# Associative scan of a hybrid layer: VectorE steps without two SBUF operands, part of the score sum on VectorE, TensorE reordered, and chunks shifted from SBUF to SBUF

## What is computed

```
def _combine(left, right, W):              # LANES = 4, hd = 32
    q = left.reshape(B, T, LANES, hd)
    k = right.reshape(B, T, LANES, hd)
    v = ((left + right) @ W).reshape(B, T, LANES, hd)
    scores = einsum('btld,btmd->btlm', q, k) * hd ** (-0.5)
    att = softmax(scores, axis=-1)
    z = einsum('btlm,btmd->btld', att, v)
    z = _rms_norm(z) / (1.0 + arange(LANES))[None, None, :, None]
    return left + z.reshape(B, T, C)

d = 1
while d < T:                               # 11 shifts: 1, 2, 4, ... 1024
    shifted = concatenate([identity rows (B, d, C), x[:, :-d]], axis=1)
    x = _combine(shifted, x, W)
    d *= 2
```

## Time and profile before

| | |
|---|---|
| time, median of 3 runs | 2099.97 us (2096.91 to 2100.51) |
| time of the profiled execution | 2098.23 us |
| its span | 2096.5 us |
| busy in the span | TensorE 1715.4 (82%), VectorE 1421.2 (68%), ScalarE 970.7 (46%), GpSimd 688.0 (33%) |
| the scan's sections, 1304.4 to 1898.5 | 44, with three to drain |

### The profile page before, as it was taken

How to read it: one execution, slowest core, us unless ns; L and a number is a source line. 1 busy time by engine, 2 the same in 40 slices (tenths; PEclk the granted TensorE clock), 3 DMA queues, 4 the chain that set the end, 5 groups by cost and what they waited for, 6 DMA issues and landing times. The chain is left out here.

```text
span 2096.5 us, 44156 instructions
## 1 busy us (share of the span) xinstructions
PE 1715.4 (82%) x14662; PEld 1126.9 (54%) x14662; DVE 1421.2 (68%) x2559; ACT 970.7 (46%) x2157; POOL 688.0 (33%) x498
## 2 busy tenths in 40 slices
PE   5699989998998999899974565899999999994374
PEld 3234333333333433334344554888888888884373
DVE  7777777777787777777624125688888888884222
ACT  4166666776676677676632112233333333332120
POOL 5300000000000000000013432677777777763532
PEclk9599999999999999999965786999999999997587
DMA  3200000000000000000007215122222222212523
GB/s 109 77 17 18 17 11 17 18 17 11 18 17 11 18 17 17 11 17 18 2 21 245 72 46 147 31 81 80 80 80 80 80 80 80 80 50 82 192 69 101
DMA packets 171652, 117.20 MB, mean 56 GB/s; under 512 B 10940, under 2 KB 161852, under 8 KB 171208
## 3 DMA queue, kind: packets, MB, share of 16 engines
q1 hardware_dynamic: 167368, 106.33, 17.3%
q0 software_dynamic: 4096, 8.46, 1.1%
HBM read 63.98 MB, written 50.72 MB: 55 GB/s over the span
## 5 line engine op out<-in xcount | busy, mean ns | idle before, releaser
L557 DVE TENSOR_REDUCE chunk_max<-ps_max 128x1 f32<-128x512 f32 (+3 forms) x1280 | 698.5, 603 | 211.2 <-PE ps_max L663 123.3
L606 ACT ACTIVATE probs<-ps_s 128x512 f32<-128x512 f32 (+3 forms) x1280 | 599.6, 547 | 317.2 <-PE ps_s L655 163.8
L636 PE MATMUL ps_s<-Qs,Ks 50*128 50x512 bf16 (+3 forms) x1280 | 379.3, 357 | 70.7 <-DVE chunk_max L557 50.7
L646 PE MATMUL ps_max<-Ks,Qs 48*128 48x512 bf16 (+3 forms) x1280 | 385.8, 360 | 13.1 <-POOL a_ident L499 10.5
L706 PE MATMUL ps_o<-probs,Vp 128*32 128x512 f32 (+3 forms) x2560 | 349.9, 571 | 11.4 <-ACT O_sb L589 11.1
L514 POOL TENSOR_TENSOR A_b<-A_newton,b_tile 128x128 f32<-128x128 f32 x32 | 14.6, 455 | 917.5 <-ACT A_newton L613 917.5
L1424 POOL TENSOR_TENSOR lane_products<-L,q 128x1024 f32<-128x1024 f32 x132 | 309.5, 2376 | 4.0 <-DMA L<-scanned 4.0
L636 PEld LDWEIGHTS ps_s<-Qs,Ks 50*128 50x128 bf16 x1280 | 103.1, 94 | 311.2 <-DVE chunk_max L557 247.1
L1479 DVE TENSOR_TENSOR weighted<-exp_scores,psV_s 128x4096 f32<-128x4096 f32 x44 | 194.2, 4413 | 0.2 <-issue 0.2
L1437 POOL TENSOR_TENSOR q<-L,z_normed 128x1024 f32<-128x1024 f32 x44 | 141.6, 3218 | 144.7 <-DVE z_normed L1459 144.7
L1558 PE MATMUL psS<-ident,lane_products 128*128 128x128 f32 x1408 | 169.4, 279 | 23.7 <-POOL lane_products L1424 23.7
(11 more groups left out here) (224 smaller groups left out, 2375.0 us busy)
## 6 DMA issues: line engine op xcount, KB each, us to landing
scanned<-q SPq DMA_DIRECT2D x44, 512.0 KB
L<-scanned SPq DMA_DIRECT2D x44, 512.0 KB
m_w<-in_L_ffn_w_dram SPq DMA_DIRECT2D x32, 512.0 KB
Qs<-q_parts SPq DMA_DIRECT2D x192, 32.0 KB
Ks<-k_parts SPq DMA_DIRECT2D x192, 32.0 KB
dispatched<-m_blank SPq DMA_DIRECT2D x2, 2080.0 KB
m_blank<-dispatched SPq DMA_DIRECT2D x16, 260.0 KB
routed<-m_blank SPq DMA_DIRECT2D x2, 2048.0 KB
```

The costliest lines, as they stand in the source:

```text
L557: nc.vector.tensor_reduce(out, scores[:, 0:w], axis=AX.X, op=ALU.max).then_inc(max_reduced, 1)
L606: nc.scalar.activation(dst, ps_s[(k + r) % R][:, q0:], ACT.Exp, scale=SCALE).then_inc(exp_done, 1)
L636: last = nc.tensor.matmul(ps_s[(k + r) % R][:, q0:], K[r][rows, kt * P:(kt + 1) * P], Q[r][rows, g * QW + q0:(g + 1) * QW], start=True, st ...
L646: last = nc.tensor.matmul(ps_max[(k + r) % R][:, 0:w], Q[r][rows, i * P:(i + 1) * P], K[r][rows, ck * QW:ck * QW + w], start=True, stop=no ...
```

## The change

L is no longer made through DRAM: three DMA transfers on SP copy from `c.q` (and from `ident_rows`, rows of `identity` now kept in SBUF) to `c.L[ch]`, for shifts under 128 by partitions, for larger ones by tiles. The store and the padding in `scan_inputs` are gone, and its waits with them. All four lane products run on GpSimd; the q sum moves to VectorE, which now writes Z scaled by `rs` back to `psZ` in PSUM and then adds `psZ` and L. VectorE sums the first 8 of the 32 features of each product (`part_scores`), and TensorE sums the other 24 and then adds `part_scores` in one more transpose. The factor of the lane and the epsilon term move into ScalarE's squares: four squares of 256 elements and four of 8 into a tensor of 33 columns, so that one reduction on VectorE gives the mean square. V and `weighted` go in two halves. On TensorE, `sum_u(1)` moves ahead of `turn_z`.

```
@@ scan_inputs, SP @@
-            sp.dma_start(ident_row[:], identity...broadcast_to([P, D]))
+            sp.dma_start(c.ident_rows[:], identity...broadcast_to([P, D]))
-            for t in scanned: (stores of the padding, 4)
-            for ch in range(SC):
-                sp.wait_ge(q_copied, ch + 1)
-                sp.dma_start(padded_rows(scanned[0], ch), c.q[:, ch]).then_inc(q_stored, 16)
-            sp.wait_ge(padded, 16 * B * len(scanned))
-            sp.wait_ge(q_stored, 16 * SC)
@@ scan, SP @@
+            def shift_in(ch, shift):
+                left, own = c.L[ch], c.q[:, ch]
+                first = ch % (SC // B) == 0
+                before = None if first else c.q[:, ch - 1]
+                if shift < P:
+                    moves = [(left[shift:], own[:P - shift]), (left[:shift, 1:], own[P - shift:, :CW - 1]),
+                             (left[:shift, 0], c.ident_rows[:shift] if first else before[P - shift:, CW - 1])]
+                else:
+                    n = shift // P
+                    def come(rows):
+                        source = c.ident_rows[rows].unsqueeze(1).broadcast_to([P // 2, n, D])
+                        return left[rows, :n], source if first else before[rows, CW - n:]
+                    lower, upper = slice(0, P // 2), slice(P // 2, P)
+                    if n < CW:
+                        moves = [(left[:, n:], own[:, :CW - n]), come(lower), come(upper)]
+                    else:
+                        (to, source), last = come(lower), come(upper)
+                        moves = [(to[:, :n // 2], source[:, :n // 2]), (to[:, n // 2:], source[:, n // 2:]), last]
+                for to, source in moves:
+                    sp.dma_start(to, source).then_inc(l_loaded[ch], 16)
             for ch in range(SC):
-                sp.dma_start(c.L[ch][:], padded_rows(scanned[0], ch, SHIFTS[0])).then_inc(l_loaded[ch], 16)
+                shift_in(ch, SHIFTS[0])
             for s in range(NS - 1):
                 for ch in range(SC):
                     sp.wait_ge(x_new, s * SC + ch + 1)
-                    (store to scanned, wait, load of L)
+                    shift_in(ch, SHIFTS[s + 1])
@@ GpSimd @@
-                if reached(g, 3): (q sum)
                 if head:
+                    for l in range(LA):
+                        last = lane_product(ch, l, lane_products[ch % 2])
+                    last.then_inc(p_done, 1)
@@ VectorE @@
                 if reached(g, 3):
                     dve.wait_ge(rs_done, g - 2)
+                    psZ = psZ * rs                                        .then_inc(z_done, 1)
+                    dve.wait_ge(z_done, g - 2)
+                    c.q[:, (ch - 3) % SC] = psZ + c.L[(ch - 3) % SC]      .then_inc(x_new, 1)
-                if head: (lane product 0)
                 if reached(g, 1):
+                    dve.wait_ge(p_done, g)
+                    nc.vector.tensor_reduce(part_scores[:], lane_products[v][:, :, :, 0:PART]...).then_inc(part_done, 1)
                     (maximum, subtraction, total as before)
+                    for half in range(2):
+                        dve.wait_ge(v_in_psum, (g - 1) * 2 + (half + 1))
+                        weighted[v][:, rows] = ... (2048 elements)        .then_inc(weighed, 1)
                 if reached(g, 2):
                     dve.wait_ge(squared, g - 1)
+                    mean_sq = tensor_reduce(squares[u] over 33)           .then_inc(ms_done, 1)
@@ ScalarE, order now @@
 copy of scores; exp; copy_z(0); copy_u(0)
+wait total_done; 4 squares of total (128x8 each)
 copy_z(1); copy_u(1)
+wait z_in_psum of both halves; 4 squares of psZ (128x256 each)
 wait ms_done; Ln; Exp
@@ TensorE @@
-                    for d in range(LW): (32 transposes into psS)
+                    for d in range(PART, LW): (24 transposes into psS)
+                    pe.wait_ge(part_done, g)
+                    nc.tensor.matmul(psS[:, 0:P], part_scores[:], c.ident[:], start=False, stop=True, is_transpose=True)
 ...
                     sum_z(range(HC, CW))
-                    wait(pe, z_done, g - 2)
+                    sum_u(1)
+                    wait(pe, x_new, g - 2)
                     turn_z(0)
                     turn_z(1)
-                    sum_u(1); wait weighed(g-1); V of 8 tiles
+                    for half in range(2):
+                        wait(pe, weighed, g * 2 + (half - 1))
+                        pe.wait_ge(uT_copied, g * 2 + (half + 1))
+                        V of 4 tiles
```

More of the change, by code:

```diff
@@ L1340, in _, with scan @@
                     last.then_inc(ready, 1)
-def scan(nc, c, scanned):
+def scan(nc, c):
     LA, LW, CE = LANES, W_LANE, CW * D
@@ L1362, in scan @@
         weighted = [sb(f"weighted{u}", [P, ROWS, LA, LW]) for u in range(2)]
-        z_normed = sb("z_normed", [P, CW, D])
-        squares = sb("z_squares", [P, ROWS, LW])
+        squares = [sb(f"z_squares{u}", [P, CW, LA, LW + 1]) for u in range(2)]
         zT = sb("zT", [P, CE])
         scores_T = sb("scores_T", [P, P])
+        part_scores = sb("part_scores", [P, LA * ROWS])
         best = sb("best_score", [P, LA * CW])
@@ L1527, in section @@
                     copy_u(0)
+                if reached(g, 1):
+                    act.wait_ge(total_done, g)
+                    wait(act, ms_done, g - 2)
+                    for l in range(LA):
+                        nc.scalar.activation(squares[v][:, :, l, LW], total[:, l, :], ACT.Square,
+                                             scale=(l + 1) * RMS_EPS ** 0.5)
                 if reached(g, 2):
                     copy_z(1)
[L1530 to L1536, removed]
                 if head:
@@ L1539, in section @@
                 if reached(g, 2):
+                    act.wait_ge(z_in_psum, (g - 2) * 2 + 2)
+                    for l in range(LA):
+                        last = nc.scalar.activation(squares[u][:, :, l, 0:LW],
+                                                    psZ[:].rearrange("p (j l d) -> p j l d", l=LA, d=LW)[:, :, l, :],
+                                                    ACT.Square, scale=(l + 1) * LW ** -0.5)
+                    last.then_inc(squared, 1)
+                if reached(g, 2):
                     act.wait_ge(ms_done, g - 1)
-                    nc.scalar.activation(log_ms[:], lane_ms[:], ACT.Ln).then_inc(rs_log, 1)
+                    nc.scalar.activation(log_ms[:], mean_sq[:], ACT.Ln).then_inc(rs_log, 1)
                     act.wait_ge(rs_log, g - 1)
@@ L1607, in section @@
                 if head:
-                    sum_u(1)
-                    wait(pe, weighed, g)
-                    for j in range(CW):
-                        if j % HC == 0:
-                            pe.wait_ge(uT_copied, g * 2 + j // HC + 1)
-                        last = nc.tensor.matmul(psV[:, j * D:(j + 1) * D], c.UT[u][:, j * P:(j + 1) * P], c.S[:, 0, :],
-                                                start=True, stop=True)
-                    last.then_inc(v_in_psum, 1)
+                    for half in range(2):
+                        wait(pe, weighed, g * 2 + (half - 1))
+                        pe.wait_ge(uT_copied, g * 2 + (half + 1))
+                        for j in range(half * HC, (half + 1) * HC):
+                            last = nc.tensor.matmul(psV[:, j * D:(j + 1) * D], c.UT[u][:, j * P:(j + 1) * P],
+                                                    c.S[:, 0, :], start=True, stop=True)
+                        last.then_inc(v_in_psum, 1)
             chunks(pe, section)
```

115 lines of the change are left out of this document (41 added, 74 removed).

## The result

The changed kernel takes 2158.0 us, median of 4 runs (2151.32 to 2160.98), against 2098.9 of 4 runs before (2096.91 to 2100.51): ratio 1.0285, 95% interval 1.0263 to 1.0306, or 59 us more. The profiled execution took 2157.89, its span is 2156.1.

What follows compares the result with a forecast made beforehand. No engine was full, so dependences bound the kernel. Slow first loads (4 x 21.8 us), 40 periods of 13.34 and a tail of 18.2 put the last q sum at 1953.1, not 1898.5: +54.6 on 2098.2 gives 2153 us, range 2104 to 2195.

Steps and rivals of the forecast that it cites:

- loads on one engine: Before the first section: each chunk's 127-partition move for shift 1 falls to one DMA engine, 21.8 us a chunk, four in sequence.
- the cycle through the part sum: Each section: last score matmul waits for VectorE's part sum, behind Z and q sum; period 13.34 us, 0.23 above 13.11.
- 172 ns a row: First loads: one engine's time for a 4096-byte row, from 7.5 ns fixed and 24.7 GB/s; 127 rows take 21.8 us.
- the term of 87 us: Start of the scan: the four chunks' first loads, one after another on one engine, 4 x 21.8 us.
- rival D: First loads: a lone engine is slower than a sixteenth of sixteen, 36.4 us a chunk, +58, 2211 us; chance 0.04.
- -6 to +14: Steady sections: the forecast's margin in us for 40 periods of 13.2 to 13.7 instead of 13.34.
- Steps 1 to 4: One section from part sum's end: TensorE to squares 6.65, mean square 9.17, Ln and Exp 9.73, next part sum 13.34 us.
- the old 13.11: Mean section in us before the change, in pairs of 12.4 and 13.8, attributed to dependences and locks between VectorE and GpSimd.
- Rival C: Steady sections: TensorE's 2.3 us standstills lower the granted clock, a tenth of 6.5 us at half clock, +27, 2180; chance 0.04.
- Shift 4: L loads of 124 partitions in the scan: on 4 engines the move takes 5.5 us, hidden under the cover.
- the cover of 13.39: Steady L loads: time that hides a load; forecast said one above 13 us would cost its excess on every section.
- Leaving DRAM earns nothing: Steady L loads: the old load's 4.2 us was already hidden by 9 us, so avoiding DRAM gains nothing there.

Runs made afterwards that it cites:

- e1: The changed kernel with shift 1's move of 127 partitions cut into 112 and 15: 2117.0 us, ratio to before 1.009.
- e10: The kernel before with the SBUF-to-SBUF shifts exactly as in the change, 127 partitions in one transfer: 2139.91 us, ratio 1.0199.
- e9: e1 with shift 1's 127 partitions dealt as 124 and 3 instead of 112 and 15: 2123.18 us, one run.
- e2: e1 with VectorE's part sum moved ahead of Z and the q sum: 2015.39 us, ratio 0.9612.
- e3: e1 without a part sum, TensorE summing all 32 features of the scores: 2036.94 us, ratio 0.9711.
- e6: e5 with Z written to SBUF instead of PSUM, so the q sum has two SBUF operands: 2056.47 us, ratio 0.9787.
- e7: The kernel before with SBUF-to-SBUF shifts alone, transfers cut as in e5: 2098.11 us, ratio 0.9988.
- e5: e2 with shifts under 16 dealt as 112 partitions and the rest, other shifts' large moves halved: 2007.93 us, ratio 0.9565.

## Why the prediction was right, step by step

It said 2153; 2158.0 was measured. The two mechanisms of the sum, loads on one engine and the cycle through the part sum, are those that the runs show; a third, the clock, was left out of it. Point by point, in the profiled execution (T(g) is the end of the part sum in section g):

| | forecast | measured |
|---|---|---|
| first transfer issued | 1298.7 | 1297.40 |
| one chunk of shift 1 | 21.8 | 19.8 |
| L of chunk 3 | 1388.3 | 1380.6 |
| from there to T(4) | 13.0 | 13.8 |
| T(4) | 1401.3 | 1394.4 |
| a section | 13.34 | 13.39 |
| long sections, T(4) to T(44) | none | 6, +9.0 in all |
| T(44) | 1934.9 | 1939.1 |
| last q sum ends | 1953.1 | 1957.1 |

*One engine for 127 partitions.* Right, and now shown from both sides: the share of 0.07 in the trace after, e1's 41 us and e10's 42. The rule that the prediction cited from the Trainium skill, "DMA: Bandwidth & Descriptors", section "Why a DMA increments its semaphore by 16 and not by 1", is borne out at two places: 127 at 0.07 and 124 at 0.26 (e9). For 112 with 15 the trace has only that far more than four engines work: a share of 0.77 and 182 GB/s from 1300 to 1302 in e1. *Its pace* was mis-sized: "172 ns a row" was 156 (19.83/127), 520,192 bytes in 19.83 us being 26.2 GB/s, so the term of 87 us was 79. The lone engine was a little faster than a sixteenth of the best window in the earlier trace rows (24.9), so rival D was wrong in sign. The forecast's own bounds, 2140 and 2192, are 3 to 4 us too low: its terms (20.9 to 28.7 us a chunk, -6 to +14) give 2144 and 2195. Nothing hangs on it.

*The new cycle.* Steps 1 to 4 hold to 0.06 us each. e2 and e3 show that it is the bound and why: take Z and q out of it, or the part sum, and the section falls to 11.0 or 11.65, which TensorE's own work gives. Z from PSUM to PSUM took 1.233, the value kept. That locks and a late GpSimd had set the old 13.11 was read from rows and is not shown by itself: e6 prices one lock in the new kernel, at 1.2 us a section, and e3 has the locks, the moved steps, the halves and the new order together at 11.65 against 13.11, not apart.

*Rival C, given 0.04, came true in a small form.* The forecast had the clock whole throughout, and named a clock under 1.00 between 1400 and 1930 as a sign of being wrong. It was 0.98 from 1470 to 1930: it fell in six sections of forty, for 3.4 us each, and cost 9.0 us, not 27. Had it been a term of the sum rather than a rival, the sum would have been 2162 with the chunk at 21.8, and 2154 with 19.8. The two misses nearly cancelled, so that the total came within 5 us is in part luck.

*Shift 4.* The forecast had 5.5 us a chunk. Its first load is first used 11.3 us after the q sum before it ended (GpSimd's timeline, the wait of 11.17 in full):

```profile
1444.78 9.31 POOL L1424 TENSOR_TENSOR lane_products<-L,q 128x1024 f32<-128x1024 f32 x4 [11.17 <-DMA L<-ident_rows]
```

less 2.4 of latency some 9 us. It stayed under the cover of 13.39, as forecast, but not under e2's 11.0. The work of the scan beside it is not the reason. In e9 the first chunk, ahead of the scan, began as slowly with all engines idle, 53 GB/s against 52 (windows of e9 and of the kernel after):

```profile
1298.50:1303.00 4.50, 0.00 (x0) 0.00 (x0) 0.00 (x0) 0.00 (x0) 0.00 (x0) 0.60 0.24 53
```
```profile
1434.50:1439.00 4.50, 4.37 (x39) 4.34 (x40) 2.54 (x5) 2.07 (x8) 0.00 (x0) 1.00 0.23 52
```

Only with the next chunks queued behind it did e9 come to 100 GB/s (1303 to 1321), the pace of the forecast. So the step that was mis-sized is the first half of a lone chunk; what makes it slow stays open.

*Leaving DRAM earns nothing.* Right in the steady state (e7). The first load is issued 2.8 us sooner in the trace after; 1.6 of that is the wait for the stores (from the end of the last copy of `scan_inputs` 1.0 instead of 2.6, in e7 too), the rest lies ahead of it.

The books, then: 41 for the first loads (e1); 12 for the sections, 42 of 13.39 instead of 13.11; 9 for the clock; less 3 for the early start: 59, as measured. The 12 and the 3 are rough: in e1's trace the first Z comes 5.0 us sooner than before, and the drain takes 2.9 longer.

## What to carry to other kernels

Moving work to an engine with room is safe only if it stands, in that engine's program, ahead of what it does not depend on: the same reduction, two steps earlier, took 102 us off (e2). Count the partitions of every transfer with no cover, look at the DMA share while it moves, and cut a number that leaves one engine at work (127 as 112 and 15, 41 us). With both mended, and shift 4 cut too, the same change is faster than the kernel before: ratio 0.9565 (e5). When a long share of an engine's time lies in short standstills, give the clock a term in the sum, not a rival's chance.

## What the runs showed that I had not expected

One DMA engine alone moved rows of 4096 bytes from SBUF to SBUF at 26.2 GB/s, steady over 80 us. Standstills of TensorE of 2.3 us in every 13.4 brought half clock for 3.4 us only in each fifth or sixth section, and 16 idle transposes a section, which leave 0.5 us of the gap, removed it: more instructions, 11 us less. Loads of 124 partitions, on four engines, began at 52 GB/s with the scan's engines at work and at 53 with all of them idle, and came to 100 only with more loads queued. And one VectorE step of 1.225 us with two SBUF operands costs 3.194 beside a GpSimd that works back to back (e6).
